# The -max transfers of three attentions are issued by SyncE in place of ScalarE

## What is computed

```
q, k, v = heads(x Wq + bq), heads(x Wk + bk), heads(x Wv + bv)    # 8 x 16 x 512 x 8
w = softmax(scale * q k^T)                                        # the second one causal
x = x + heads_back(w v) Wo
```

## Time and profile before

| what | us |
|---|---|
| median of 3 runs | 3156.8 (3155.18 to 3157.17) |
| span of the profiled execution, first to last instruction | 3142.6 |
| PE busy / DVE busy / ACT busy in the span | 2346.1 / 2149.6 / 1558.5 |

### The profile page before, as it was taken

The page is one execution under the profiler, slowest core; times in us unless marked ns, Lnnn a source line. Parts: engine busy times, 40 slices in busy tenths (PEclk is TensorE's granted clock), DMA queues, the critical chain, the costliest instruction groups (busy, mean ns, idle before and its releaser), DMA issues. The chain is left out here.

```text
span 3142.6 us, 49400 instructions
## 1 busy us (share of the span) xinstructions
PE 2346.1 (75%) x17438; PEld 1176.4 (37%) x17438; DVE 2149.6 (68%) x4458; ACT 1558.5 (50%) x3005; POOL 1147.9 (37%) x1200
## 2 busy tenths in 40 slices
PE   2999997877488888575656778777526937988896
PEld 1233332545244444354642333333216832233332
DVE  4888895877576666365237889999652247888784
ACT  1677773111155556233336766766312214766675
POOL 3222202434212120133344667776573443223200
PEclk9999998777599999677877988999758967899998
DMA  5111100000111210201760000000017942211110
GB/s 170 40 29 34 29 15 1 1 1 1 31 35 35 40 34 21 61 22 24 254 202 0 0 1 1 0 0 1 6 44 231 303 113 41 45 35 36 31 24 14
DMA packets 132742, 157.55 MB, mean 50 GB/s; under 512 B 20560, under 2 KB 113872, under 8 KB 131888
## 3 DMA queue, kind: packets, MB, share of 16 engines
q1 hardware_dynamic: 122832, 140.44, 17.0%
q0 software_dynamic: 6592, 13.56, 1.2%
q10 hardware_dynamic: 3072, 0.40, 0.1%
HBM read 96.09 MB, written 25.59 MB: 39 GB/s over the span
## 5 line engine op out<-in xcount | busy, mean ns | idle before, releaser
L433 DVE TENSOR_REDUCE a_mx<-banks 128x1 f32<-128x512 f32 (+3 forms) x1536 | 880.9, 617 | 279.6 <-PE banks L909 150.8
L780 ACT ACTIVATE a_prob<-banks 128x512 f32<-128x512 f32 (+3 forms) x1536 | 776.5, 545 | 418.3 <-PE banks L932 193.4
L909 PE MATMUL banks<-a_Ks,a_Qs 63*128 63x512 bf16 (+3 forms) x1536 | 511.4, 378 | 66.7 <-DVE a_mx L433 47.2
L932 PE MATMUL banks<-a_Qs,a_Ks 64*128 64x512 bf16 (+3 forms) x1536 | 520.3, 371 | 50.8 <-ACT a_prob L780 44.7
L960 PE MATMUL banks<-a_prob,a_vaug 128*32 128x256 f32 (+2 forms) x5632 | 453.1, 395 | 1.0 <-ACT a_prob L780 0.9
L2094 POOL TENSOR_TENSOR m_hc<-m_h,m_cs 128x512 f32<-128x512 f32 x256 | 332.2, 1319 | 131.8 <-DVE m_h L1959 129.0
L1959 DVE TENSOR_TENSOR_SCAN m_h<-banks,m_u 128x512 f32<-128x512 f32 x256 | 301.3, 1211 | 21.1 <-issue 21.1
L2242 PE MATMUL banks<-m_hc,kc 128*128 128x512 f32 x512 | 292.2, 655 | 9.6 <-DVE m_yf L2076 8.5
L909 PEld LDWEIGHTS banks<-a_Ks,a_Qs 63*128 63x128 bf16 x1536 | 128.5, 95 | 439.7 <-DVE a_mx L433 232.3
L2150 ACT ACTIVATE banks<-m_dt,acoef 128x512 f32<-128x512 f32 x256 | 174.9, 688 | 137.4 <-DVE m_h L1959 136.5
L932 PEld LDWEIGHTS banks<-a_Qs,a_Ks 64*128 64x128 bf16 x1536 | 138.3, 93 | 178.9 <-ACT a_prob L780 138.7
(11 more groups left out here) (411 smaller groups left out, 4518.8 us busy)
## 6 DMA issues: line engine op xcount, KB each, us to landing
c_wbuf<-in_w2e SPq DMA_DIRECT2D x71, 512.0 KB, 4.1
b_wbuf<-in_w1e SPq DMA_DIRECT2D x39, 578.0 KB, 4.3
a_Ks<-a_parts SPq DMA_DIRECT2D x288, 64.0 KB
a_Qs<-a_parts SPq DMA_DIRECT2D x288, 64.0 KB
rows_in<-in_unused SPq DMA_DIRECT2D x1, 4579.5 KB, 16.9
c_yb<-rows_in SPq DMA_DIRECT2D x71, 64.5 KB, 4.3
a_mixed_in<-rows_back SPq DMA_DIRECT2D x16, 256.0 KB, 3.8
a_Qs<-a_negm ACTq DMA_DIRECT2D x192, 2.0 KB
```

The costliest lines, as they stand in the source:

```text
L433: dve.tensor_reduce(mx[:, g % 2, col:col + 1], M[:, k % 3, 0:keys[j]], AX.X, ALU.max).then_inc(S("max_read"), 1)
L780: act.activation(prob[:, n % 8, first_query[kt]:T], Sc[:, n % 2, first_query[kt]:T], ACT.Exp, scale=scale).then_inc(S("exped"), 1)
L909: i = pe.matmul(M[:, k % 3, 0:keys[j]], Qs[lo:lo + LAST, b % 4, pair, j * P:(j + 1) * P], Ks[lo:lo + LAST, b % 4, pair, 0:keys[j]], start= ...
L932: i = pe.matmul(Sc[:, n % 2, q0:T], Ks[lo:lo + HALF, b % 4, pair, kt * P:(kt + 1) * P], Qs[lo:lo + HALF, b % 4, pair, q0:T], start=True, s ...
```

## The change

The lane that waits for the maxima and issues the two -max transfers of every group moves from ScalarE's program to SyncE's. Its waits, its due times, its transfers and their semaphore are the same.

```
@@ -780,18 +780,18 @@
-                def scalar_maxima(act):
+                def sync_maxima(sp):
                     for k, (g, m) in enumerate(order):
                         if m < 16:
                             continue
                         yield max_at(g, m) + 1.6
-                        act.wait_ge(S("max_read"), k + 1)
+                        sp.wait_ge(S("max_read"), k + 1)
                         if g:
-                            act.wait_ge(S("negmax_placed"), 32 * g)
+                            sp.wait_ge(S("negmax_placed"), 32 * g)
                         own = 2 * (g % NG)
                         for par in range(2):
                             at_row = HALF * par + LAST
-                            act.dma_start(Qs[at_row:at_row + 1, g // NG % 4, own:own + 2, :],
+                            sp.dma_start(Qs[at_row:at_row + 1, g // NG % 4, own:own + 2, :],
                                           negm[8 * par:8 * par + 8, g % 2, :]).then_inc(S("negmax_placed"), 16)
@@ -1034,7 +1034,7 @@
-                         "scalar": [scalar_core, scalar_maxima, scalar_values], "sync": [sync_set] + ([sync_corners] if corners else []),
+                         "scalar": [scalar_core, scalar_values], "sync": [sync_set, sync_maxima] + ([sync_corners] if corners else []),
```

## The result

| | before | changed |
|---|---|---|
| median of the runs, us | 3156.99 (3155.18 to 3161.72, 4 runs) | 3205.61 (3193.31 to 3209.96, 4 runs) |
| span of the profiled execution, us | 3142.6 | 3202.9 |

The change makes the kernel slower: ratio 1.0149, 95% interval 1.0124 to 1.0173. The forecast was 3168, the range 3142 to 3198: the sign was right, the size far too small, and the time lies above the range.

The account below looks back on a forecast made before the run. VectorE was taken to bound the first attention and PE the second. Span 3142.6 - 36 gain + 49 loss = 3155.6, plus 14.2 gives 3169.8, rounded to 3168 us; range 3142 to 3198.

Parts of the forecast that it names:

- The place and number of the waits: Score matmuls wait for -max pairs behind SyncE's sends in all three attentions: 15 places, 58.8 us.
- the 3.3 us from issue to landing: Assumed time for a pair on SyncE's queue to land behind sends; bounds 2.5 and 4.7 us.
- The softening: Queued VectorE tiles cover part of each wait: 0.9 us off at 8 places, 0.4 at 7, 10 us in all.
- raw lateness: Delay of first score matmuls behind late pairs before any cover is taken off: 58.8 us over the three attentions.
- the wait feeds on itself: Rival: engines restart empty after a stall and the next pair's gain is lost too; 3202 us, chance 0.15.
- The gain: ScalarE time freed per pair in the three attentions: 8.6 + 17.5 + 10 = 36 us saved.
- The base: Whole kernel: runs taken to lie 14.2 us above the profiled span of 3142.6 us.
- The signs named: Profile signs: 14 to 16 waits, shorter steady groups, first and second attention each 5 to 12 us longer, third 5 to 8 shorter.
- my sum: Whole kernel: span 3142.6 less 36 gain plus 49 loss, with 14.2 above the span: 3169.8, rounded to 3168 us.

Follow-up runs that it names:

- e6_paced: The changed kernel with the due times of the 24 sends spread as the chip takes them, so each pair falls behind 14 sends, not 20; 3126.34 us, ratio 0.9926.
- e4_split: The changed kernel with the 21 of 96 pairs that stand among sends left on ScalarE, the rest issued by SyncE; 3126.17 us, ratio 0.9937.
- e5_fill: The changed kernel with 16 spare matmuls ahead of the wait in late groups of the first two attentions and the first's group 0; 3180.26 us, ratio 1.0108.
- e8_deep: The changed kernel with eight semaphores for the sends in place of four, so up to eight are in flight; 3205.88 us, ratio 1.0154.
- e9_late: The kernel before, all pairs on ScalarE, with six pairs of the first attention's late groups due 4 us later; 3182.75 us, ratio 1.0083.

## Why the prediction was right in sign and wrong in size

**The place and number of the waits: right.** 16 waits of 59.0 us against 58.8, at the places named (the 58.8 holds 16 places too, as group 24 of the third attention with its 0.3 was left out of the count of 15; it waited 0.2), and the 3.3 us from issue to landing stand against 2.6 to 3.3 in the first two attentions. e6_paced and e4_split show that the order is their cause: with the order mended or the 21 pairs taken out of it, the loss is gone. The lateness of single groups was up to 1.9 us off either way, and that these misses cancel is luck.

**The softening: wrong.** The step "VectorE has one or two finished tiles to read, and where VectorE is the limit that much is no loss" took 10 us off, 6.3 of them in the first attention, and there nothing came of it: with group 0 the late groups grew by 28.2 us against a raw lateness of 25.5. Tiles that were covered would also show as shorter groups behind the wait; in e5_fill, where the clock stays up, those are 0.3 us longer in all. In the second attention 28.0 lies between 26.9 with softening and 29.7 without, and decides nothing. The step's condition was not met: "where VectorE is the limit" was read from the steady groups, but the late ones stand beside the work for the next batch, and group 8 had VectorE busy for 10.57 of 12.62 us and PE for 12.48. The timeline adds that VectorE did read its queued tiles, but got a new one only at 207.05, 1.07 us after PE began again: what was covered at the front of the wait is lost at its end. That this is the reason is argued from these two views of one group; no run tests it.

**The cost behind the wait: missing.** The rival "the wait feeds on itself" had the right sign and a size near the result, but as it was put (a higher landing time and a smaller gain) it isn't what happened. A lower clock after each wait was in no case of mine. It costs 10.7 us in the first attention by the groups' own lengths, and e5_fill removes it; in the second, where part of it is given back, e5_fill's attention is 5 to 7 us shorter than the changed kernel's.

**The gain: oversized.** The price per group was not too high: steady groups gained 0.50 us in the first attention (0.45 taken) and 1.04 in the second (0.70 taken). The count was. Of the second's 25 groups those beside projections kept 13.19 us, and those behind a late group or held otherwise gained less. Measured 6.5 and 12.4 us for 8.6 and 17.5. In e4_split, without the waits, the net gain of the two attentions is 17.9 us. In the third attention 10 us were foreseen; 6.1 were measured, and the spread of unchanged kernels leaves open how much of that is gain.

**The base: misread, without harm.** I took the 14.2 us between span and median for what lies around the span. As 3142.6 and 14.2 give back the median of before, the forecast is none the worse for it. But the profile of the changed kernel has a time of 3204.73 at a span of 3202.9: 1.8 us lie around it. So the profiled execution of before was about 12 us shorter than the median, and the stretch "between" alone moves by 15 us from one execution to the next. That is why the spans differ by 60.3 us and the medians by 48.6.

**The signs named.** The waits and the steady groups came as named (10.75 and 9.54 us for 10.8 and 9.9). The attentions did not: the first was to be longer by 5 to 12 us and was by 22.6, behind a start 9.7 later, and the second, 5 to 12 too, by 15.6.

**The sum again.** Of the 48.6 us, my sum had 13 (49 less 36), rounded to 11. Missing were 10 for the softening, 10.7 for the clock in the first attention, 11.1 of gain (2.1, 5.1 and 3.9 in the three attentions, the clock's share in the second among it) and 1 of lateness (2.7 more in the first, 1.7 less in the second): 45.8. In the profiles the attentions and the stretch between the first two grew by 46.6 us of the 60.3; that 45.8 also lies near the 48.6 of the medians is in part chance. The terms come from one profile of each kernel; by the spreads above, those of the second attention are good to some 4 us and those of the third to some 6.

**Left open.** Whether the third attention gains, and how much, is not told. Why the stretch between the second and third attention differs between executions was not tried. How much of the second attention's loss is the clock and how much the later sends is not told apart by e5_fill, which moved both.

## What to carry to other kernels

Before a cheap instruction is moved to an "idle" engine, read what its queue holds at that moment, on the chip and not by plan: here 21 of 96 pairs stood behind sends, and leaving these on ScalarE while SyncE took the other 75 beat both versions. Where due times that an order is built from are closer than the chip can keep, the order is wrong for whatever is merged into it. A wait of 2 to 4 us on PE is to be priced with its clock afterwards, and tiles queued for another engine are not to be counted as cover where that engine is not the limit. And a stretch is to be compared with kernels that leave it alone, more than one of them, before a gain is read from it.

## What the runs showed of the hardware

- After PE idle times of 2.2 us (changed kernel, 205.98) and 2.65 us (e9_late, 198.54) the granted clock was at 0.50 for about 6 us, and the group that ran then took 15.0 us for 12.6. With PE kept busy by spare matmuls (e5_fill) it stayed at 1.00. The Trainium skill, page "TensorE: Matmul & The Clock Gate", section "HAM oscillation — how this bites in real kernels", tells of the same sequence, a wait for a DMA and then matmuls at half clock; these traces agree.
- A pair of two transfers of 2 KB took 2.4 us from issue to landing alone on SyncE's queue (changed kernel, steady groups), 2.6 to 3.3 us behind four sends of 64 KB in flight (changed kernel, late groups of the first two attentions), 4.2 to 8.2 us at the late groups with up to eight in flight (e8_deep), and 4.8 us on ScalarE's queue while SyncE was sending (e9_late, 193.70 to 198.54).
